# The first layer's output bias is added behind each chunk's norm, and the fourth chunk's transposes stand four side steps later

## The chip, the cores and the metric

The kernel runs on one core of a Trainium2 chip. The metric is the device time in microseconds of one execution. Three executions of the kernel before took 730.15, 731.93 and 731.92 us, median 731.92 us.

## The reference

Two transformer layers on an input `x` of 2 x 1024 tokens of width 256, all float32. Each layer normalizes `x`, feeds the result to an attention and to a gated feed-forward block, and adds both to `x`:

```python
xn = _layernorm(x)
x = x + _L0_attn_ref(xn, ...) + _L0_ffn_ref(xn, ...)
xn = _layernorm(x)
x = x + _L1_attn_ref(xn, ...) + _L1_ffn_ref(xn, ...)
```

The part around the change is layer 0. Its attention is linear, with 16 heads of 16, and its last operation adds a bias row `o_b` to every token:

```python
qp = elu(q) + 1.0;  kp = elu(k) + 1.0
kv = einsum('bhsd,bhse->bhde', kp, v)
z = einsum('bhsd,bhd->bhs', qp, kp.sum(axis=2))[..., None]
attn = einsum('bhsd,bhde->bhse', qp, kv) / (z + EPS)
return out @ o_w.T + o_b
```

Its feed-forward block uses three ternary weights, `clip(round(w / s), -1, 1) * s` with `s` the mean of `|w|`, as `down(silu(up(x)) * gate(x))`. Layer 1 has softmax attention with rotary positions and a Hadamard-rotated feed-forward block; the change does not touch it.

## The kernel before, in words

The 2048 tokens are four chunks of 512, held in `X` as 16 tiles of 128 tokens on the partitions. Every float32 product is done in two or three float32r passes, with operands split in a high and a low part (`XH`, `XL` for the normalized input, `W0H`, `W0L` for the weights of layer 0).

All engines run one list of pieces that `work_order` writes out. Each engine walks the same list and issues only its share of each piece; semaphores hold them together. So the place of a piece in the list sets the order on every engine at once. Generators feed the list: `layernorm` (one per chunk), `ternary` (one per ternary weight), `attention0` through `side0`, and `ffn` as the main loop. The start of the kernel, before `half` and the first `gate`, is written by a short loop of `FIRST` = 12 side steps. The change is in that loop.

The pieces that matter here:

- `ln_stats n`: VectorE takes mean and variance of chunk n (L1128, L1132, L1135), and GpSimd raises the variance to the power -0.5 (`rstd`, L1592).
- `ln_norm n`: VectorE writes the normalized chunk to `XC` in four instructions (L1144), out of `X`.
- `ln_turn n`: TensorE transposes the four tiles of `XC` (L807), ScalarE copies the two banks to `XH` (L1437), VectorE subtracts that from the banks to get `XL` (L1150). This is "the norm's turn".
- `bias 0 c`: GpSimd adds the row `OB` to the chunk c in `X` (L1601, 128x1024). It waits for the load of `OB` and for the chunk's four `ln_norm` instructions, since these read `X`.
- `kv_in t`, `kv_sum t`, `kv_out t`: key and value projection of token tile t. TensorE projects, VectorE adds biases (L1215 for `zk`, L1216 for `ve`, each from a bank in PSUM and the row `BKV` in SBUF), ScalarE makes the exponential (`ek`, L1454 and L1456), VectorE combines `zk` and `ek` (L1235, both in SBUF), and TensorE accumulates keys times values (L841). The banks 0 and 1 are used in turn.
- `q0 c m`: half of the query projection of a chunk. VectorE L1230, ScalarE `zs` (L1466, L1468), GpSimd adds the two (`QP`, L1613, both in SBUF).
- `tern_abs n`, `tern_scale n`, `tern_cut n j`: the ternary weight n (`TU`, `TG`, `TD`). ScalarE sums absolute values (L1446), VectorE makes the threshold (L1173 to L1176), compares all 2048 columns with it (L1178), and finishes in two halves (L1186, both inputs in SBUF).
- `gate`, `up` of the feed-forward block: ScalarE L1508, VectorE L1267 and L1280, then ScalarE rounds the product to `hh` (L1516), and GpSimd makes its low part `hl` (L1646, both inputs in SBUF).

GpSimd also adds the bias for layer 1 in the same place of each later norm (`bias 1 c` in `ln1`); that is not changed.

Of the kernel before, what the change touches and what calls it, by code (L numbers as in the profile page):

```python
# [49 lines left out]
class Ring:  # L50
# [5 lines left out]
    def next(self):  # L56
        self.i = (self.i + 1) % len(self.slots)
        return self.slots[self.i]
# [12 lines left out]
def work_order():  # L71
# [3 lines left out]
    def put(*piece):  # L75
        order.append(piece)
# [217 lines left out]
    sd0 = side0()  # L294
    next(sd0)
    next(ln0[2])
    next(sd0)
    for n in range(FIRST):
        if n < 10:
            next(tn)  # L300
        next(sd0)
        if n < 4:
            next(ln0[2 if n == 0 else 3])
        if n > 7:
            put("bias", 0, n - 8)
    put("half")
    put("load_down")
    put("load_ob1")
# [138 lines left out]
def program(nc, x_d, wa0, tern, wa1, wo1, wf1, cols_d, bkv_d, cos_d, sin_d, had_d, mask_d, ident_d, pad_d, sel_d, wl_d, ob_d, wsd_d, y_d):  # L447
    with ExitStack() as ctx:
# [134 lines left out]
        def o_slots(p):  # L583
# [7 lines left out]
            return (f"oe{o}", n), (f"num{i}", done), (f"rc{o}", n), (f"rs{o}", n)  # L591

        order = work_order()
        block = ctx.enter_context(nc.Block())

# [1209 lines left out]
```

## Time and profile before

| | |
|---|---|
| median of three executions | 731.92 us |
| profiled execution, its own time | 732.69 us |
| its span | 730.9 us |
| TensorE busy | 699.4 us, 96% of the span |
| VectorE busy | 529.2 us, 72% |
| ScalarE busy | 432.9 us, 59% |
| GpSimd busy | 288.2 us, 39% |
| mean granted TensorE clock | 0.986 |

Busy shares are means over the whole span. In the page's slices TensorE is at nine tenths or more nearly everywhere but in the first four slices (0 to 73 us), where it is at seven or eight tenths and VectorE at seven or eight as well. The change lies in those slices. The 18 to 70 us stretch has to be read from the timeline and the chain of waits, one instruction at a time, since there the engines hand work to one another every few tenths of a microsecond.

### The profile page before, as it was taken

Reading aid. Unit: us, or ns where it says so; the run is one execution under the profiler, and the core shown is the slowest. Engines: PE = TensorE matmul, PEld = TensorE weight load, DVE = VectorE, ACT = ScalarE, POOL = GpSimd, SP = SyncE. Lnnn points to the kernel's source line nnn. Section 1 sums busy time; section 2 is a strip of 40 time slices with the busy share of each in tenths; the row PEclk is TensorE's granted clock in tenths of the full one; section 3 lists DMA queues with packets and bytes.
Section 4 is the critical chain, followed back from the end, with each engine's and each line's share of the span. In section 5 each row is a group of like instructions: output and inputs, shape, how many; then the busy total and the mean of one; then the engine's idle time right before and its main releaser. Section 6 shows DMA issues by size and latency. Waiting matters only on the chain.

```text
span 730.9 us, 11063 instructions
## 1 busy us (share of the span) xinstructions
PE 699.4 (96%) x4246; PEld 441.5 (60%) x4246; DVE 529.2 (72%) x864; ACT 432.9 (59%) x592; POOL 288.2 (39%) x261
## 2 busy tenths in 40 slices
PE   7787999989998999999999999999999999999998
PEld 6576898977776888677676773333333333333445
DVE  7878875655668677678778788888886388888315
ACT  3363434446543522432332338999998999999883
POOL 2237944348665632542543431122333224332410
PEclk8999999989999999999999999999999999999999
DMA  7157001012025562423111022344443344433321
GB/s 266 55 187 231 1 1 58 1 26 91 1 87 173 167 208 87 144 70 105 59 59 35 25 67 71 126 140 160 123 143 126 100 146 146 145 94 91 105 79 58
DMA packets 25848, 74.14 MB, mean 101 GB/s; under 512 B 4620, under 2 KB 5996, under 8 KB 24964
## 3 DMA queue, kind: packets, MB, share of 16 engines
q1 hardware_dynamic: 21268, 65.37, 26.9%
q0 software_dynamic: 3808, 7.60, 3.6%
q8 instruction: 34, 0.56, 0.3%
q10 hardware_dynamic: 720, 0.48, 0.2%
q14 instruction: 18, 0.15, 0.1%
HBM read 54.54 MB, written 23.06 MB: 106 GB/s over the span
## 4 chain that ended last, share of the span: by engine, by line
PE 78%; DVE 10%; issue 5%; ACT 4%; POOL 3%; DMA 1%; DVEq 0%; ACTq 0%; POOLq 0%
PE PS L769 22%; PE PS L1038 17%; PE PS L1024 12%; PE PS L775 12%; PE PS L1007 6%; PE PS L997 5%; DVE mx L1342 1%; DVE bst L1128 1%; PE PS L903 1%; PE PS L858 1%; POOL hl L1646 1%; DVE sg L1280 1%; DVE rot L1325 1%; ACT XD L1432 1%; DMA X<-in_x 1%
## 5 line engine op out<-in xcount | busy, mean ns | idle before, releaser
L1554 ACT ACTIVATE P<-PS 128x1024 f32<-128x1024 f32 x256 | 249.0, 1024 | 30.0 <-PE PS L1024 29.7
L1349 DVE TENSOR_REDUCE mx<-PS 128x1 f32<-128x512 f32 x300 | 189.1, 682 | 32.3 <-PE PS L1007 30.6
L1342 DVE TENSOR_REDUCE mx<-PS 128x2 f32<-128x1024 f32 x106 | 124.8, 1220 | 36.6 <-PE PS L997 36.3
L1038 PE MATMUL PS<-P,VV 128*32 128x512 f32 x1024 | 136.4, 605 | 0.1
L1646 POOL TENSOR_TENSOR hl<-sg,hh 128x512 fp32r<-128x512 f32 x64 | 85.2, 1332 | 126.1 <-ACT hh L1524 75.8
L1024 PEld LDWEIGHTS PS<-QS,KS 64*128 64x128 f32 x512 | 48.4, 183 | 121.3 <-ACT P L1554 109.5
L1024 PE MATMUL PS<-QS,KS 64*128 64x512 f32 x512 | 116.4, 455 | 0.9 <-DVE mx L1342 0.6
L1007 PE MATMUL PS<-KM,QM 64*128 64x512 f32 x300 | 81.0, 395 | 0.0
L1510 ACT ACTIVATE sg<-PS,cols 128x512 f32<-128x512 f32 x32 | 22.0, 688 | 86.9 <-PE PS L769 86.9
L769 PE MATMUL PS<-XH,UGH 128*128 128x512 f32 x128 | 54.4, 425 | 3.7 <-DVE sg L1278 2.0
L769 PE MATMUL PS<-XL,UGH 128*128 128x512 f32 x128 | 50.5, 394 | 0.0
L769 PE MATMUL PS<-XH,UGL 128*128 128x512 f32 x128 | 50.0, 391 | 0.0
L1516 ACT ACTIVATE hh<-sg 128x512 fp32r<-128x512 f32 x32 | 20.1, 630 | 49.3 <-DVE sg L1280 49.3
L1655 POOL TENSOR_TENSOR sg<-sg,us 128x512 f32<-128x512 f32 x24 | 30.9, 1286 | 35.7 <-ACT us L1519 35.7
L1038 PEld LDWEIGHTS PS<-P,VV 128*32 128x32 f32 x1024 | 20.2, 108 | 39.8 <-issue 35.3
L997 PE MATMUL PS<-KM,QM 64*128 64x512 f32 x212 | 39.9, 448 | 0.8 <-DVE mx L1342 0.6
L1007 PEld LDWEIGHTS PS<-KM,QM 64*128 64x128 f32 x300 | 38.0, 185 | 3.4 <-DVE mx L1349 0.6
L775 PE MATMUL PS<-DH,hh 128*128 128x256 f32 x128 | 38.0, 297 | 0.0
L775 PE MATMUL PS<-DL,hh 128*128 128x256 f32 x128 | 36.1, 282 | 0.0
L775 PE MATMUL PS<-DH,hl 128*128 128x256 f32 x128 | 36.1, 282 | 0.0
L769 PEld LDWEIGHTS PS<-XH,UGH 128*128 128x128 f32 x128 | 24.0, 188 | 19.6 <-issue 10.8
L775 PE MATMUL PS<-TD,hh 128*128 128x256 f32 x128 | 34.0, 300 | 1.6 <-POOL hl L1646 1.6
(212 smaller groups left out, 1358.6 us busy)
## 6 DMA issues: line engine op xcount, KB each, us to landing
QM<-scr_q SPq DMA_DIRECT2D x16, 512.0 KB, 4.3
KM<-scr_k SPq DMA_DIRECT2D x16, 512.0 KB, 5.3
QS<-scr_q SPq DMA_DIRECT2D x16, 512.0 KB, 4.5
KS<-scr_k SPq DMA_DIRECT2D x16, 512.0 KB, 5.4
scr_q<-spl SPq DMA_DIRECT2D x24, 256.0 KB, 3.2
scr_k<-spl SPq DMA_DIRECT2D x24, 256.0 KB, 3.4
scr_o<-OE POOLq DMA_DIRECT2D x14, 256.0 KB, 2.8
stg<-in_tern SPq DMA_DIRECT2D x3, 1024.0 KB, 6.1
```

Of the source, the lines that this page charges most:

```text
L769: i = e.matmul(out, l, r, start=start and j == 0, stop=stop and j == len(pairs) - 1)
L775: i = e.matmul(out[:, r * 256:r * 256 + 256], l, x, start=first and r == 0 and j == 0, stop=last and j == len(pairs) - 1, skip_group_check ...
L997: e.matmul(bank[b + h], QM[p % 2][hr, qt * 128:(qt + 1) * 128], KM[p % 2][hr, chunk(half)], start=True, stop=True).then_inc(q["mt"], 1)
L1007: e.matmul(bank[b], QM[p % 2][hr, qt * 128:(qt + 1) * 128], KM[p % 2][hr, chunk(half)], start=True, stop=True).then_inc(q["mt"], 1)
L1024: i = e.matmul(bank[b + h], KS[p % 2][hr, kt * 128:(kt + 1) * 128], QS[p % 2][hr, chunk(half)], start=True, stop=True)
L1038: i = e.matmul(PS[32 * c:32 * c + 32, 7, :], v_head(8 * b + kt, 2 * j + c // 2), P[s % 4][:, chunk(c // 2 + 2 * (c % 2))], start=(kt == 0) ...
L1342: e.tensor_reduce(mx[p % 2][:, :, qt, half], PS[:, b:b + 2, :], AX.X, ALU.max).then_inc(q["mx"], 2)
L1349: e.tensor_reduce(mx[p % 2][:, h, qt, half:half + 1], bank[b], AX.X, ALU.max).then_inc(q["mx"], 1)
L1510: e.activation(s[:, :], bank[b], ACT.Silu, scale=col("wsg", m) if layer else su).then_inc(q["t"], 1)
L1554: e.activation(P[s % 4][:, half * 1024:(half + 1) * 1024], PS[:, b:b + 2, :].rearrange("p b n -> p (b n)"), ACT.Exp).then_inc(q["ex"], 1)
L1646: e.tensor_tensor(hl[f % 4][:, :], sg[f % 3][:, :], r32(hh[f % 4][:, :]), ALU.subtract).then_inc(q["hl"], 1)
L1655: e.tensor_tensor(s[:, :], s[:, :], us[f % 4][:, :], ALU.mult).then_inc(q["h"], 1)
```

## The change

The list of pieces is the same but for the places of five of them. The first three biases stand right behind `ln_norm 2`, where chunks 0 and 1 have long been normalized; the fourth stands behind `ln_norm 3`. Before, the four stood at the end of the start, behind the query and key work. And `ln_turn 3` is put at step 6 of the loop and no more at step 3 (counted from 0): behind `kv_in 6`, and no more behind `q0 0 1`.

```diff
     next(sd0)
     next(ln0[2])
+    for c in range(3):
+        put("bias", 0, c)
     next(sd0)
     for n in range(FIRST):
         if n < 10:
             next(tn)
         next(sd0)
-        if n < 4:
+        if n in (0, 1, 2, 6):
             next(ln0[2 if n == 0 else 3])
-        if n > 7:
-            put("bias", 0, n - 8)
+        if n == 2:
+            put("bias", 0, 3)
     put("half")
```

The changed file is two lines longer, so that the lines of the engines' code have numbers two higher in it (L1603 is the old L1601).

The first place is on GpSimd, from the third norm's `rstd` to the first `hl`. `X<-X,OB` is the bias; `QP` is the query add. Before:

```order
L1592 TENSOR_TENSOR rstd_144<-rstd_144,MINUS_HALF 128x4
L1592 TENSOR_TENSOR rstd_145<-rstd_145,MINUS_HALF 128x4
L1613 TENSOR_TENSOR QP<-zs_93,QP 128x512
L1613 TENSOR_TENSOR QP<-zs_94,QP 128x512
L1613 TENSOR_TENSOR QP<-zs_93,QP 128x512
L1601 TENSOR_TENSOR X<-X,OB 128x1024
L1613 TENSOR_TENSOR QP<-zs_94,QP 128x512
L1601 TENSOR_TENSOR X<-X,OB 128x1024 x3
L1646 TENSOR_TENSOR hl_110<-sg_118,hh_106 128x512
```

The same stretch now:

```order
L1594 TENSOR_TENSOR rstd_144<-rstd_144,MINUS_HALF 128x4
L1603 TENSOR_TENSOR X<-X,OB 128x1024 x3
L1594 TENSOR_TENSOR rstd_145<-rstd_145,MINUS_HALF 128x4
L1615 TENSOR_TENSOR QP<-zs_93,QP 128x512
L1603 TENSOR_TENSOR X<-X,OB 128x1024
L1615 TENSOR_TENSOR QP<-zs_94,QP 128x512
L1615 TENSOR_TENSOR QP<-zs_93,QP 128x512
L1615 TENSOR_TENSOR QP<-zs_94,QP 128x512
L1648 TENSOR_TENSOR hl_110<-sg_118,hh_106 128x512
```

Three biases moved ahead of the fourth norm's `rstd`, one between the first two query adds, and none is left ahead of `hl`.

The second place is on ScalarE, around the sum over the second ternary weight, `TG`. `XH` is the fourth norm's turn. Before:

```order
L1466 ACTIVATE zs1_94<-PS,MINUS_QB_62 128x512
L1468 ACTIVATE zs1_94<-zs1_94 128x512
L1437 ACTIVATE XH_68<-PS 128x512 x2
L1446 ACTIVATE TG_77,s16_53<-stg0_121 128x2048
L1454 ACTIVATE ek0_84<-zk0_80 128x256
L1456 ACTIVATE ek0_84<-ek0_84 128x256
L1454 ACTIVATE ek1_85<-zk1_81 128x256
L1456 ACTIVATE ek1_85<-ek1_85 128x256
L1454 ACTIVATE ek2_86<-zk2_82 128x256
L1456 ACTIVATE ek2_86<-ek2_86 128x256
L1454 ACTIVATE ek3_87<-zk3_83 128x256
```

Now:

```order
L1468 ACTIVATE zs1_94<-PS,MINUS_QB_62 128x512
L1470 ACTIVATE zs1_94<-zs1_94 128x512
L1448 ACTIVATE TG_77,s16_53<-stg0_121 128x2048
L1456 ACTIVATE ek0_84<-zk0_80 128x256
L1458 ACTIVATE ek0_84<-ek0_84 128x256
L1456 ACTIVATE ek1_85<-zk1_81 128x256
L1458 ACTIVATE ek1_85<-ek1_85 128x256
L1456 ACTIVATE ek2_86<-zk2_82 128x256
L1458 ACTIVATE ek2_86<-ek2_86 128x256
L1439 ACTIVATE XH_68<-PS 128x512 x2
L1456 ACTIVATE ek3_87<-zk3_83 128x256
```

The two copies to `XH` moved from ahead of the sum over `TG` to behind the exponentials of token tile 6 (`ek2`).

The third place is on VectorE, between the comparison of `TG` and its first half cut. Before:

```order
L1178 TENSOR_SCALAR TG<-stg_121,s_53 128x2048
L1215 TENSOR_TENSOR zk_82<-PS,BKV 128x256
L1216 TENSOR_TENSOR ve_90<-PS,BKV 128x2x128
L1235 SCALAR_TENSOR_TENSOR zk_81<-zk_81,ek_85 128x256
L1186 SCALAR_TENSOR_TENSOR TG<-stg_121,s_53,TG 128x1024
L1215 TENSOR_TENSOR zk_83<-PS,BKV 128x256
```

Now:

```order
L1180 TENSOR_SCALAR TG<-stg_121,s_53 128x2048
L1217 TENSOR_TENSOR zk_82<-PS,BKV 128x256
L1218 TENSOR_TENSOR ve_90<-PS,BKV 128x2x128
L1237 SCALAR_TENSOR_TENSOR zk_81<-zk_81,ek_85 128x256
L1152 TENSOR_TENSOR XL<-PS,XH 128x512 x2
L1188 SCALAR_TENSOR_TENSOR TG<-stg_121,s_53,TG 128x1024
L1217 TENSOR_TENSOR zk_83<-PS,BKV 128x256
```

The two subtractions for `XL` moved in ahead of the cut; they had stood ahead of the `zk` of token tile 4.

## Rows read from the trace of the kernel before

**Rows 1.** Busy time by stretch; columns: us, then PE, PEld, DVE, ACT, POOL, clock, DMA
```profile
80.00:100.00 20.00, 20.00 (x139) 18.59 (x138) 14.94 (x28) 6.18 (x12) 14.58 (x8) 1.00 0.01 1
```

**Rows 2.** Chain that ended last; columns: start us, us, engine and line
```profile
72.18 0.73 PE PS L858 x4
```

**Rows 3.** Timeline of GpSimd, 15 to 63 us; columns: start us, us, engine, line, operation
```profile
15.03 2.98 POOL L1592 TENSOR_TENSOR rstd<-rstd,MINUS_HALF 128x4 f32<-128x4 f32 x1 [4.62 <-DVE rstd L1135]
...
54.70 8.10 POOL L1601 TENSOR_TENSOR X<-X,OB 128x1024 f32<-128x1024 f32 x3
...
57.06 5.74 POOL L1601 TENSOR_TENSOR X<-X,OB 128x1024 f32<-128x1024 f32 x2
...
62.77 3.48 POOL L1646 TENSOR_TENSOR hl<-sg,hh 128x512 fp32r<-128x512 f32 x2
```

**Rows 4.** Timeline of VectorE, 20 to 26 us
```profile
20.91 1.37 DVE L1144 TENSOR_SCALAR XC<-X,mv,rstd 128x256 f32<-128x256 f32 x4
...
22.87 0.41 DVE L1235 SCALAR_TENSOR_TENSOR zk<-zk,ek 128x256 f32<-128x256 f32 x1
23.20 0.42 DVE L1215 TENSOR_TENSOR zk<-PS,BKV 128x256 f32<-128x256 f32 x1
...
23.87 0.41 DVE L1235 SCALAR_TENSOR_TENSOR zk<-zk,ek 128x256 f32<-128x256 f32 x1
25.03 1.29 DVE L1150 TENSOR_TENSOR XL<-PS,XH 128x512 fp32r<-128x512 f32 x2 [0.75 <-ACT XH L1437]
```

**Rows 5.** Timeline at 75.9 us, GpSimd and VectorE side by side
```profile
75.87 1.31 POOL L1646 TENSOR_TENSOR hl<-sg,hh 128x512 fp32r<-128x512 f32 x1
75.93 1.53 DVE L1235 SCALAR_TENSOR_TENSOR zk<-zk,ek 128x256 f32<-128x256 f32 x1
```

**Rows 6.** Instructions of L1144 and L1178; durations in ns, min/median/max
```profile
L1144 DVE TENSOR_SCALAR XC<-X,mv,rstd x16: 404/406/414, 9.0 to 33.9; 128x256 f32<-128x256 f32 x16
...
L1178 DVE TENSOR_SCALAR TG<-stg,s x1: 1287/1287/1287, 42.0 to 42.0; 128x2048 fp32r<-128x2048 f32 x1
```

**Rows 7.** Timeline of all engines, 34 to 42 us
```profile
34.26 2.43 POOL L1613 TENSOR_TENSOR QP<-zs,QP 128x512 f32<-128x512 f32 x1 [1.32 <-ACT zs L1468]
34.27 1.28 DVE L1186 SCALAR_TENSOR_TENSOR TU<-stg,s,TU 128x1024 fp32r<-128x1024 f32 x1
...
36.96 0.63 ACT L1468 ACTIVATE zs<-zs 128x512 f32<-128x512 f32 x1
37.50 1.07 ACT L1437 ACTIVATE XH<-PS 128x512 fp32r<-128x512 f32 x2
...
38.45 1.91 ACT L1446 ACTIVATE TG<-stg 128x2048 fp32r<-128x2048 f32 x1
...
41.24 0.42 DVE L1235 SCALAR_TENSOR_TENSOR zk<-zk,ek 128x256 f32<-128x256 f32 x1 [0.18 <-ACT ek L1456]
```

**Rows 8.** Timeline of ScalarE and VectorE, the third turn and the cut of TG
```profile
24.10 0.42 ACT L1456 ACTIVATE ek<-ek 128x256 f32<-128x256 f32 x1
...
24.42 1.07 ACT L1437 ACTIVATE XH<-PS 128x512 fp32r<-128x512 f32 x2
...
44.12 0.42 ACT L1456 ACTIVATE ek<-ek 128x256 f32<-128x256 f32 x1
...
44.22 1.28 DVE L1186 SCALAR_TENSOR_TENSOR TG<-stg,s,TG 128x1024 fp32r<-128x1024 f32 x1
```

**Rows 9.** Timeline of VectorE and ScalarE, 57 to 66 us
```profile
57.93 2.62 DVE L1178 TENSOR_SCALAR TD<-stg,s 128x2048 fp32r<-128x2048 f32 x1
...
60.47 0.68 DVE L1280 TENSOR_TENSOR sg<-sg,PS 128x512 f32<-128x512 f32 x1
...
61.17 0.63 ACT L1516 ACTIVATE hh<-sg 128x512 fp32r<-128x512 f32 x1 [3.03 <-DVE sg L1280]
...
62.94 2.17 DVE L1186 SCALAR_TENSOR_TENSOR TD<-stg,s,TD 128x1024 fp32r<-128x1024 f32 x1
...
65.03 0.68 DVE L1267 SCALAR_TENSOR_TENSOR sg<-sg,PS 128x512 f32<-128x512 f32 x1
```

## The prediction

> **What bounds the kernel now.** I read the stretches first, then the chain of waits, then the timeline of the stretch that the change touches. From 80 to 100 us TensorE is busy for 20.00 of 20.00 us [rows 1], and the page's slices keep it at nine tenths or so until the end. Up to there it isn't the bound: the chain of waits runs through VectorE, with pieces of ScalarE and GpSimd, and goes over to TensorE at 72.18 us [rows 2]. So I treat whatever moves that handover as moving the end by the same amount, and nothing that the change does lies behind it. The sum is therefore a walk from 18 to 72 us along VectorE and ScalarE. The times are those of the trace of before; "x late" means against it.
>
> What the walk needs most is how GpSimd and VectorE get in each other's way. At 75.87 GpSimd starts an add of two SBUF tiles, and at 75.93 VectorE starts its L1235, also with two SBUF inputs, and takes 1.53 us [rows 5] where it takes 0.41 alone [rows 4]. GpSimd's add ends at 77.18, L1235 at 77.46: it began in earnest about when the add was done, and ended 0.28 behind it. The same at 57.93: the comparison L1178 takes 2.62 us [rows 9] against 1.29 [rows 6], because a bias had begun at 57.06 [rows 3]. VectorE wins the other way round: at 34.27 it begins a cut, and GpSimd's query add takes 2.43 us [rows 7]. Instructions that read PSUM and one SBUF tile show no such stretching: L1280 at 60.47, beside a bias, takes its 0.68 [rows 9].
>
> **The biases at their new place.** The third norm's rstd ends at 15.03 + 2.98 = 18.01 [rows 3]. The waits of the first two biases have long been met. A bias every 2.36 us (57.06 less 54.70 [rows 3]) gives starts at 18.0, 20.35 and 22.7; the third waits for the third norm, done at 22.28 [rows 4], so it doesn't wait. It ends at 25.06. VectorE reaches the first L1235 at 22.87 [rows 4], 0.17 behind it. With 0.06 ahead GpSimd had the port in [rows 5]. Then L1235 ends at 25.06 + 0.28 = 25.34 and not at 23.28, and what follows it is 2.07 late. Nothing absorbs that: the next L1215 at 23.20 feeds ScalarE's exponential, behind which stand XH and then XL at 25.03 [rows 4], where VectorE waits for ScalarE as it is. So +2.07.
>
> The other end: if the gap behind rstd, which no row shows, is 0.2 us or more, VectorE passes first. Its L1235 runs at 22.87, the third bias gets the port at about 23.1 and ends at 25.5, and it is the second L1235, at 23.87, that is held to 25.8. XL follows at 25.72 and not at 25.03: +0.70. I take +2.07, since 0.17 is more than the 0.06 that did for GpSimd in [rows 5], and keep +0.70.
>
> **The fourth bias.** It stands behind the first query add, which ended at 34.26 + 2.43 = 36.69 [rows 7], so it runs from 36.7 to 39.1 (all plus the shift so far). It holds up the L1235 of tile 3 until 39.3. Behind that stand L1215 and L1216 of tile 5, two thirds of a microsecond at 0.33 each, so that VectorE is ready for the next L1235 at 39.9. That one needs ScalarE's exponential, which by the next paragraph is there at 40.3. Cost 0, with 0.4 to spare; if that cover goes, up to 2.
>
> **The turn, where it leaves.** Before, ScalarE goes from the exponential of zs (36.96) to the two XH copies at 37.50 and to the sum over TG at 38.45 [rows 7]. Now the sum starts at 37.50: 0.95 sooner. All behind it follows: the exponentials of tile 4, the L1235 that waits for them (41.24 with 0.18 of idle time before it [rows 7]), the threshold, the comparison of TG. By the paragraph above VectorE can follow to 40.29. TensorE gets its key work for tile 4 sooner, since it no longer waits there for the fourth norm, so it holds nobody. So -0.95. VectorE's two XL instructions leave idle time there, which is worth nothing.
>
> **The turn, where it comes in.** VectorE has to do the two XL between the L1235 of tile 5 and the first cut of TG at 44.22 [rows 8]. They need XH, which stands on ScalarE behind the exponential of tile 6 that begins at 44.12. Such an XH begins 0.32 behind the start of the exponential (24.10 to 24.42) and XL 0.61 behind XH (24.42 to 25.03 [rows 4, 8]), so XL at 44.12 + 0.93 = 45.05. Two XL keep VectorE for 1.21 (1.29 less the overlap with what follows), and the cut starts at 46.26: +2.04. From there to the handover VectorE and ScalarE work through the cuts, the query adds and the sum over TD in line, so nothing gives it back. Together the turn costs 1.09. The lower bound of this term is 0 for the arrival (it would be hidden if VectorE had 2 us to wait there, which [rows 8] deny), the upper one 2.04 plus what a later bank costs TensorE, which has the keys of tile 7 to do meanwhile and is not waited for.
>
> **The biases at their old place.** Three of them kept GpSimd from 54.70 to 62.80 [rows 3]. Two instructions of VectorE paid. The comparison for TD took 2.62 at 57.93; at 1.29 it saves 1.33, and L1280 at 60.47, hh at 61.17 and the cut at 62.94 move up by as much [rows 9]. That cut took 2.17 because two hl had piled up behind the biases and started at 62.77 [rows 3]; alone it takes 1.28 [rows 8], a saving of 0.89. Not all of it: the second hl can now begin 0.07 behind its hh, at 61.17 - 1.33 + 0.63 + 0.07 = 60.54, takes 1.31 [rows 5], and ends at 61.85, while the cut wants the port at 61.61. By the end of L1235 in [rows 5] VectorE gets going some 0.13 ahead of the recorded end, so that costs about 0.11, and 0.78 stay. So -1.33 - 0.78 = -2.11, and L1267 at 65.03 is up by as much. Nothing of GpSimd's stands behind this but the hl, fold and butterfly pieces in their old order.
>
> **Sum.** +2.07 - 0.95 + 2.04 - 1.33 - 0.78 = +1.05. The profiled execution took 732.69, 0.77 above the median of 731.92. On its own scale the kernel comes to 733.7, on that of the median to 733.0 us.
>
> **Rivals.**
>
> (1) VectorE slips ahead of the third bias. For it: 0.17 us is all the room there is, and no row shows how soon GpSimd starts something behind an rstd. Against it: other adds of GpSimd follow one another without a gap (54.70 + 2.36 = 57.06). Sum: 0.70 in place of 2.07, hence -0.32 and 731.6 us.
>
> (2) Slower: the norm's own instructions are held by the biases too. At 20.91 VectorE begins four XC instructions while the second bias runs, until 22.7. Held up to there, they end at 24.0; the third bias waits for them and runs from 24.05 to 26.4; L1235, reached at 24.5, ends at 26.7. What follows it is then 3.45 late and not 2.07, the sum +2.4, the time 734.3 us. It decides if XC takes more than 0.41 beside a bias. Against it: sixteen XC lie between 404 and 414 ns [rows 6], those of the first norm beside a GpSimd rstd. But that one is 4 columns wide, so it is no full proof. The Trainium skill, in "SBUF — State Buffer", section "Who interferes with whom", lists tensor_scalar among the operations that can enter a mode that takes both ports of VectorE, and says that whichever engine issues first has the shared pair for the whole instruction; by that the XC would be held and the time would be this rival's, and by its sentence that an instruction with one SBUF input outside such a mode doesn't contend, it would be my forecast. The trace speaks for the second: L1144 needs 1.37 us for 4 x 256 columns [rows 4], L1178 1.29 for 2048 [rows 6], so L1144 runs at about half the pace of the one and is not in the fast mode.
>
> (3) Faster: the turn's arrival is hidden, because the chain at 43 to 48 us is in truth ScalarE's or TensorE's, and (1) as well. Sum -0.32 - 2.04 = -2.36, time 729.6 us. For it: VectorE idles in most microseconds of this stretch for a little. Against it: the cut at 44.22 begins with no idle time before it [rows 8].
>
> There is one more tie, at 34.26 and 34.27 [rows 7]: both engines shift alike there, so VectorE should win it again. If GpSimd does, VectorE's cut is late by a query add, about 1.1, in any of the cases.
>
> **Chances.** The forecast 0.42; (1) 0.26; (2) 0.10; (3) 0.10; the tie lost or something not seen 0.12, half to each side. What a measurement of this kernel can tell from no change is about 0.3%, 2.2 us. The forecast and (1) lie within it; (2) is just above, (3) just below it. That makes faster 0.15, same 0.69, slower 0.16. The range goes from just above (3) to just above (2), 729.8 to 734.7 us; the forecast's own is 732.2 to 733.7.
>
> **What would show it.** In the profile after: one L1237 near 22.9 us with 2.4 to 2.5 us of duration (forecast), or a second one at 23.9 with about 1.9 (rival 1); XC at 20.9 still at 0.41 each (else rival 2); the sum over TG 0.95 nearer to the exponential of zs; VectorE waiting 0.8 us for XH ahead of XL at about 46; no instruction of TD's comparison above 1.3 us and its first cut below 1.4; TensorE's first L860 behind which it stays busy at about 73.2 us and not 72.18. I am wrong if that handover moves by more than 2 us, or if it moves as said and the end doesn't follow.

## The result: slower by 4.1 us

| | before | after |
|---|---|---|
| median | 731.93 us (5 runs, 730.15 to 732.48) | 735.98 us (5 runs, 734.87 to 737.67) |
| profiled execution, its own time | 732.69 us | 736.19 us |
| span | 730.9 us | 734.3 us |
| handover to TensorE | 72.18 us | 75.06 us |

The ratio is 1.0058, with a 95% interval of 1.0039 to 1.0077. The forecast was 733.0 us with a range of 729.8 to 734.7, and 0.16 for "slower by over 0.3%". That is what came, and the median lies outside the range.

VectorE's timeline from the second norm's `XL` to `XL` of the third, in the profile after. Columns: start us, us, engine, line, operation.

```profile
16.84 1.28 DVE L1152 TENSOR_TENSOR XL<-PS,XH 128x512 fp32r<-128x512 f32 x2
18.03 2.14 DVE L1165 TENSOR_SCALAR s<-cols 128x2 f32<-128x2 f32 x1
20.09 0.16 DVE L1166 TENSOR_SCALAR s16b<-cols 128x8 f32<-128x8 f32 x1
20.16 2.31 DVE L1167 TENSOR_SCALAR MINUS_QB<-cols 128x2 f32<-128x2 f32 x1
22.38 0.16 DVE L1169 TENSOR_SCALAR MASK<-MASK 128x8 f32<-128x8 f32 x1
22.46 0.41 DVE L1217 TENSOR_TENSOR zk<-PS,BKV 128x256 f32<-128x256 f32 x1
...
23.12 1.37 DVE L1146 TENSOR_SCALAR XC<-X,mv,rstd 128x256 f32<-128x256 f32 x4
...
25.08 2.14 DVE L1237 SCALAR_TENSOR_TENSOR zk<-zk,ek 128x256 f32<-128x256 f32 x1
27.15 0.41 DVE L1217 TENSOR_TENSOR zk<-PS,BKV 128x256 f32<-128x256 f32 x1
...
28.98 1.29 DVE L1152 TENSOR_TENSOR XL<-PS,XH 128x512 fp32r<-128x512 f32 x2 [0.76 <-ACT XH L1439]
```

And GpSimd's timeline in the same stretch and at the biases' old place:

```profile
17.76 4.69 POOL L1603 TENSOR_TENSOR X<-X,OB 128x1024 f32<-128x1024 f32 x2
24.57 2.37 POOL L1603 TENSOR_TENSOR X<-X,OB 128x1024 f32<-128x1024 f32 x1 [2.12 <-DVE XC L1146]
...
60.76 1.29 POOL L1648 TENSOR_TENSOR hl<-sg,hh 128x512 fp32r<-128x512 f32 x1 [1.41 <-ACT hh L1518]
65.62 1.28 POOL L1648 TENSOR_TENSOR hl<-sg,hh 128x512 fp32r<-128x512 f32 x1 [3.58 <-ACT hh L1518]
```

Four things are to be seen. L1165 and L1167, two tensor_scalar instructions 128x2 wide of the piece `signs`, take 2.14 and 2.31 us beside the first two biases; the eight-column L1166 slips between the two biases at 0.16. So the first key add (L1217) comes at 22.46, where it came at 20.24 before. The four XC at 23.12 come after the second bias, so no bias runs beside them in this profile, and the third bias waits for them. It starts at 24.57, half a microsecond ahead of the key sum L1237 at 25.08, which then takes 2.14 us where it takes 0.41 alone; that is the hold forecast for the key sum at the old 22.87 [rows 4]. And the hl of GpSimd start at 60.76 and 65.62, right behind their hh, not in a heap as in [rows 3].

The rest of the start, where each line answers to one of [rows 7 to 9]:

```profile
41.09 2.18 DVE L1237 SCALAR_TENSOR_TENSOR zk<-zk,ek 128x256 f32<-128x256 f32 x1
...
44.23 0.45 DVE L1237 SCALAR_TENSOR_TENSOR zk<-zk,ek 128x256 f32<-128x256 f32 x1 [0.29 <-ACT ek L1458]
...
48.07 1.29 DVE L1152 TENSOR_TENSOR XL<-PS,XH 128x512 fp32r<-128x512 f32 x2 [0.76 <-ACT XH L1439]
49.28 1.28 DVE L1188 SCALAR_TENSOR_TENSOR TG<-stg,s,TG 128x1024 fp32r<-128x1024 f32 x1
```
```profile
40.92 0.63 ACT L1470 ACTIVATE zs<-zs 128x512 f32<-128x512 f32 x1
41.46 1.90 ACT L1448 ACTIVATE TG<-stg 128x2048 fp32r<-128x2048 f32 x1
...
47.14 0.42 ACT L1458 ACTIVATE ek<-ek 128x256 f32<-128x256 f32 x1
47.46 1.06 ACT L1439 ACTIVATE XH<-PS 128x512 fp32r<-128x512 f32 x2
```
```profile
62.99 1.28 DVE L1180 TENSOR_SCALAR TD<-stg,s 128x2048 fp32r<-128x2048 f32 x1
64.19 0.68 DVE L1282 TENSOR_TENSOR sg<-sg,PS 128x512 f32<-128x512 f32 x1
...
66.67 1.32 DVE L1188 SCALAR_TENSOR_TENSOR TD<-stg,s,TD 128x1024 fp32r<-128x1024 f32 x1
67.91 0.67 DVE L1269 SCALAR_TENSOR_TENSOR sg<-sg,PS 128x512 f32<-128x512 f32 x1
```

The first fence is VectorE around the comparison of TG, the second ScalarE beside it, the third VectorE at TD. The sum over TG starts 0.54 behind the exponential, without the XH copies between. VectorE waits for XH before XL at 48.07, and the cut of TG comes at 49.28. TD's comparison takes 1.28 and its first cut 1.32 us.

Each step can be read off as the lateness of one instruction against the first profile, and the difference from one row to the next is what the step cost:

| what | before | after | late | step | forecast |
|---|---|---|---|---|---|
| first key add, L1215 | 20.24 | 22.46 | +2.22 | +2.22 | 0 |
| key add of tile 2 | 23.20 | 27.15 | +3.95 | +1.73 | +2.07 |
| key sum of tile 4, L1235 | 41.24 | 44.23 | +2.99 | -0.96 | -0.95 |
| first cut of TG, L1186 | 44.22 | 49.28 | +5.06 | +2.07 | +2.04 |
| L1280 behind TD's comparison | 60.47 | 64.19 | +3.72 | -1.34 | -1.33 |
| L1267 behind TD's cut | 65.03 | 67.91 | +2.88 | -0.84 | -0.78 |
| handover, L858 | 72.18 | 75.06 | +2.88 | 0 | 0 |
| an hh behind the handover, L1516 | 87.61 | 92.00 | +4.39 | +1.51 | 0 |
| an hh behind the fifth norm, L1516 | 166.37 | 169.82 | +3.45 | -0.94 | 0 |

The last two steps go with TensorE's clock; for the first of them an experiment below shows it, the second was not tested. TensorE by stretches of the profile after; columns: stretch and its us, then PE, PEld, DVE, ACT, POOL busy with instructions, granted clock, DMA share, GB/s. First the handover:

```profile
75.06 1.27 PE L860 MATMUL PS<-kvb,QP 128*128 128x136 f32 x4 [2.85 <-DVE at L1249]
```
```profile
76.00:80.00 4.00, 4.00 (x15) 3.21 (x15) 2.10 (x7) 0.95 (x2) 4.00 (x3) 0.71 0.00 0
```

TensorE had idled for 2.85 us and then had a mean granted clock of 0.71 over 76 to 80 us: part of that time it ran at 1.2 GHz and part at 2.4. A matmul of 512 columns took 0.63 us at the lower level where it took 0.39 in the profile before:

```profile
76.56 0.63 PE L771 MATMUL PS<-XL,TU 128*128 128x512 f32 x1
```
```profile
72.98 0.39 PE L769 MATMUL PS<-XL,TU 128*128 128x512 f32 x1
```

In the profile before, the idle time at this place was 1.42 us, and the stretch had clock 1.00:

```profile
76.00:80.00 4.00, 4.00 (x25) 3.55 (x24) 2.81 (x5) 2.25 (x5) 4.00 (x3) 1.00 0.01 4
```

The same thing the other way round stands at the fifth norm: ten microseconds of it in the profile before, and the ten of the same work, 4 us later, in that after:

```profile
154.00:164.00 10.00, 8.75 (x42) 7.58 (x41) 4.37 (x11) 3.30 (x7) 3.75 (x3) 0.66 0.15 31
```
```profile
158.00:168.00 10.00, 8.53 (x45) 7.47 (x46) 5.24 (x14) 3.98 (x8) 4.30 (x3) 0.83 0.17 53
```

There the clock was 0.66 before and 0.83 after, and 0.94 us came back. From there to the end nothing moves by more than about 0.1 us; the span ends 3.4 us later.

### The profile page after: what moved, and what is told of

It reads as the page before. It is cut to its first block, busy times and chain, and to the rows that moved or that the text cites. A ratio compares the mean times of both kernels' runs of the same rounds, so it can differ in the third digit from the quotient of the medians.

```text
span 734.3 us, 11063 instructions
## 1 busy us (share of the span) xinstructions
PE 699.3 (95%) x4246; PEld 441.0 (60%) x4246; DVE 534.5 (73%) x864; ACT 432.8 (59%) x592; POOL 286.3 (39%) x261
## 4 chain that ended last, share of the span: by engine, by line
PE 76%; DVE 11%; issue 5%; ACT 4%; POOL 3%; DMA 1%; DVEq 0%; ACTq 0%; POOLq 0%
PE PS L771 21%; PE PS L1040 17%; PE PS L1026 12%; PE PS L777 11%; PE PS L1009 6%; PE PS L999 5%; DVE bst L1130 1%; DVE mx L1344 1%; PE PS L905 1%; PE PS L860 1%; DVE XL L1152 1%; POOL hl L1648 1%; DVE sg L1282 1%; DVE rot L1327 1%; ACT XD L1434 1%
## 5 line engine op out<-in xcount | busy, mean ns | idle before, releaser
L1040 PEld LDWEIGHTS PS<-P,VV 128*32 128x32 f32 x1024 | 20.2, 108 | 39.8 <-issue 35.3
```

The source lines that it names most:

```text
L1040: i = e.matmul(PS[32 * c:32 * c + 32, 7, :], v_head(8 * b + kt, 2 * j + c // 2), P[s % 4][:, chunk(c // 2 + 2 * (c % 2))], start=(kt == 0) ...
```

## The experiments

All were timed over 5 to 12 executions against the kernel before on the same chip. "Late" is again against the first profile of before.

**The biases alone.** The turn is left where it was.

```diff
+    for c in range(3):
+        put("bias", 0, c)
     next(sd0)
     for n in range(FIRST):
         ...
         if n < 4:
             next(ln0[2 if n == 0 else 3])
-        if n > 7:
-            put("bias", 0, n - 8)
+        if n == 2:
+            put("bias", 0, 3)
```

> The kernel before with the four biases at their new places, and the fourth turn where it was. Theory A (two small tensor_scalar instructions of the piece signs, 2 columns wide, and then one L1235 are held by the early biases): VectorE's first key add is late by 2.4 us, what follows the first L1235 by 4.2, the place where the bias left gives 2.2 back, so the handover to TensorE moves by +2.0 and the end by 2 to 3.5 us. Rival B (the turn's move is what costs): the handover moves by less than 0.5 us and the end too.

Measured: 734.6 us against 731.83, ratio 1.0038 [1.0023, 1.0053]. VectorE again shows the two held instructions, and the key sum:

```profile
18.42 2.15 DVE L1165 TENSOR_SCALAR s<-cols 128x2 f32<-128x2 f32 x1
...
20.55 2.31 DVE L1167 TENSOR_SCALAR MINUS_QB<-cols 128x2 f32<-128x2 f32 x1
...
25.47 2.15 DVE L1237 SCALAR_TENSOR_TENSOR zk<-zk,ek 128x256 f32<-128x256 f32 x1
```

TD's comparison takes 1.29 us. The handover comes at 74.36, +2.18 (forecast +2.0), and the span ends 2.5 us later. This profile runs 0.39 us behind that of the changed kernel already at L1165 (18.42 against 18.03); 2.18 - 0.39, and 1.10 for the turn (next experiment), make up the 2.88 of the changed kernel. So the biases cost most of it. Rival B falls.

**The turn alone.**

```diff
-        if n < 4:
+        if n in (0, 1, 2, 6):
             next(ln0[2 if n == 0 else 3])
```

> The kernel before with only the fourth turn moved. Theory A: the sum over TG starts 0.95 us sooner, the first cut of TG 1.1 later, the handover 1.1 later and the end 1 to 2.5 us later, all of it still in TD's comparison at 2.6 us. Rival B: the handover and the end move by 3 us or more.

Measured: 732.58 us against 731.83, ratio 1.0009 [0.9996, 1.0021]: 0.7 us, and the interval takes in nothing and 1.5. The profile has to be read with care, since the handover stands at 72.06, 0.12 sooner than before. But the first key add comes at 19.02 and not at 20.24, in code that is the same up to there. From the first key add to the handover it is 53.04 us here and 51.94 in the profile before: the turn costs 1.10, as the -0.96 and +2.07 above. What differs at the start is TensorE's clock, here in this kernel and then in the one before, over the same stretches:

```profile
14.00:16.00 2.00, 2.00 (x14) 2.00 (x13) 1.93 (x7) 2.00 (x4) 1.10 (x1) 0.68 0.28 115
16.00:18.00 2.00, 2.00 (x17) 1.91 (x16) 2.00 (x3) 1.54 (x2) 1.88 (x1) 1.00 0.00 0
```
```profile
14.00:16.00 2.00, 2.00 (x12) 2.00 (x11) 1.93 (x8) 2.00 (x4) 0.97 (x1) 0.50 0.31 127
16.00:18.00 2.00, 2.00 (x12) 2.00 (x12) 2.00 (x3) 1.64 (x2) 2.00 (x1) 0.57 0.00 0
```

Rival B falls. Theory A's 1 to 2.5 us at the end were not seen: the profile ends 0.2 us later, with the early start in it, and the size of the turn's cost in the median is only as sure as the interval.

**The changed kernel with `signs` out of the biases' way.**

```diff
-    for i in (0, 1, 0, 1, 0, 2):
+    for i in (0, 1, 0, 1, 0):
         next(ln0[i])
+    put("signs")
+    next(ln0[2])
 ...
     next(tn)
-    put("signs")
```

> The changed kernel with the piece signs (four small tensor_scalar instructions of VectorE) ahead of the third norm's statistics, where no bias runs. Theory A: they take 0.16 us each, the first key add comes at its old time of 20.2 us, and VectorE meets the third bias at its first L1235 as the prediction said, held there for about 2 us; the handover falls by 2.1 us against the changed kernel, the end by 2 to 3.5. It also puts the four XC instructions beside the second bias for the first time. Rival C (a bias holds any tensor_scalar with its input in SBUF): XC is held for 1.5 to 1.8 us too, and of the 2.1 us less than 0.8 are left. Rival B (signs stands beside the path): no change.

Measured: 735.29 us against 731.83, ratio 1.0052 [1.0038, 1.0067], hardly less than the changed kernel. `signs` is no more held, and the first key add comes at 19.09. But the XC are. Two rows of VectorE in narrow windows, and the second bias, with the third:

```profile
19.76 0.91 DVE L1147 TENSOR_SCALAR XC<-X,mv,rstd 128x256 f32<-128x256 f32 x1
```
```profile
20.59 2.45 DVE L1147 TENSOR_SCALAR XC<-X,mv,rstd 128x256 f32<-128x256 f32 x1
```
```profile
20.48 2.41 POOL L1604 TENSOR_TENSOR X<-X,OB 128x1024 f32<-128x1024 f32 x1
23.77 2.35 POOL L1604 TENSOR_TENSOR X<-X,OB 128x1024 f32<-128x1024 f32 x1 [0.88 <-DVE XC L1147]
```

The first XC takes 0.91, up to the end of the first bias, and the second 2.45, up to the end of the second bias that started 0.11 ahead of it; the last two take 0.4 each. The third bias then stretches the key sum to 2.12. The handover comes at 74.24, 0.82 sooner than in the changed kernel and not 2.1. Theory A was right that a bias had held `signs` and wrong on the gain, since the hold only went over to the next instruction that needs the port; rival C comes near to what was seen. It is the mechanism of rival 2 of the prediction, with only the second XC held for long.

**The idle time at the handover filled.** The changed kernel, with eight matmuls of ones (16 instructions in the trace) in front of the attention step that waits there.

```diff
     def att_n(tt):
+        if tt == 3:
+            put("busy", 8, 4)
         put("att_n", tt, ps.next())
```

> The changed kernel with eight matmuls of ones (128x128, their result is written to a bank that is written anew afterwards) ahead of the attention step at the handover, where TensorE idled 2.85 us and then ran with a granted clock of 0.71 for 76 to 80 us. Theory D (the clock behind that idle time cost 1.3 to 1.5 us of the 3.5): the clock stays at 1.00 behind the handover, the ScalarE step at about 88 us comes 1.3 to 1.5 us sooner, and the end by 0.5 to 1.5 us. Rival E (the clock there costs nothing, since VectorE sets the pace until 90 us): the step at 88 us and the end stay within 0.3 us.

Measured: 735.05 us against 731.83, ratio 1.0044 [1.0029, 1.0058]; the changed kernel had 1.0058 in its own comparison. VectorE does the same up to the handover, at 75.08. Behind it the clock stays up, and the hh of the table comes at 90.50 and not at 92.00:

```profile
75.08 0.73 PE L862 MATMUL PS<-kvb,QP 128*128 128x136 f32 x4 [0.74 <-DVE at L1251]
```
```profile
76.00:80.00 4.00, 4.00 (x24) 3.45 (x23) 3.49 (x8) 1.81 (x4) 4.00 (x2) 1.00 0.02 4
```
```profile
90.50 0.63 ACT L1520 ACTIVATE hh<-sg 128x512 fp32r<-128x512 f32 x1 [1.91 <-DVE sg L1284]
```

So 1.50 us between the handover and that hh were the clock. Up to 703 us 1.4 to 1.5 of them are left (2.0 late and not 3.4 to 3.5); at 722 us TensorE then waits 0.47 for VectorE, and the span ends 1.0 sooner than that of the changed kernel (733.3 and 734.3). The profiled execution took 735.12 and not 736.19. The medians differ by 0.9 us, with intervals that overlap. Theory D holds, rival E falls.

**The kernel before once more.**

> The kernel before, unchanged, for a second profile. In its first profile TensorE's granted clock was 0.50 to 0.57 from 12 to 18 us and the first key add came at 20.2 us; in two of the experiments the clock rose sooner and the first key add came at 19.0 to 19.1. Theory F (the point at which the clock rises at the start differs from execution to execution, and nothing else does): the time is within 0.2% of before, and if this profile has the clock up at 16 us, the handover to TensorE comes at about 71 us and not at 72.2. Rival G (the start is the same in each execution of this kernel): first key add at 20.2 again.

Measured: 732.08 us against 731.86, ratio 0.9995 [0.9979, 1.0011]. The first key add came at 20.35 and the handover at 72.31, the clock being 0.50 at 16 to 18 us. So both profiles of this kernel have the late start, as rival G says, and theory F is not shown. The turn alone, whose code is the same up to there, had the early one, but that is another program. The 23 executions of before that this one was compared with lie between 730.07 and 734.60 us, so something differs from one execution to the next; no profile shows that it is this. This execution took 734.03 us: 1.0 of that is a stretch near 247 us, which the other profiles lack.

**The biases in the gaps.** The kernel before, the turn as it was.

```diff
     for n in range(FIRST):
         ...
+        if n == 0:
+            put("bias", 0, 0)
         if n < 4:
             next(ln0[2 if n == 0 else 3])
-        if n > 7:
-            put("bias", 0, n - 8)
+        if n == 2:
+            put("bias", 0, 1)
+        if n in (8, 9):
+            put("bias", 0, n - 6)
 ...
             def bias(layer, c):
                 e.wait_ge(q["lnn"], 4 * (4 * layer + c + 1))
+                if layer == 0 and c == 0:
+                    e.wait_ge(q["kvk"], 2)
```

> The kernel before with its biases set where VectorE does nothing that a bias holds: chunk 0 behind the second key sum (GpSimd waits for it, about 24.3 to 26.7 us), chunk 1 between the first two query adds (36.7 to 39.1), chunks 2 and 3 where the first two stood. The turn stays. Theory A (only instructions that need the shared port pay): no instruction of VectorE before 50 us is longer than before by more than 0.2 us, but for 0.3 us at the key sum of tile 3; TD's comparison takes 1.3 us and its first cut under 1.4; the handover comes 2.0 to 2.2 us sooner than before, and the median falls by 1.5 to 2.5 us, to 729.5 to 730.5. Rival H (the early biases cost through something else than the port, as the waits of the query adds): the handover moves by less than 1 us.

Measured: 730.09 us against 731.86, ratio 0.9969 [0.9954, 0.9984], 12 and 23 runs: faster than both kernels. GpSimd with its four biases, and VectorE at the instructions that could pay:

```profile
24.54 2.38 POOL L1607 TENSOR_TENSOR X<-X,OB 128x1024 f32<-128x1024 f32 x1 [6.65 <-issue]
...
36.79 2.37 POOL L1607 TENSOR_TENSOR X<-X,OB 128x1024 f32<-128x1024 f32 x1
...
51.26 2.40 POOL L1607 TENSOR_TENSOR X<-X,OB 128x1024 f32<-128x1024 f32 x1
...
54.87 2.39 POOL L1607 TENSOR_TENSOR X<-X,OB 128x1024 f32<-128x1024 f32 x1
57.23 1.27 POOL L1652 TENSOR_TENSOR hl<-sg,hh 128x512 fp32r<-128x512 f32 x1
```
```profile
26.80 1.29 DVE L1182 TENSOR_SCALAR TU<-stg,s 128x2048 fp32r<-128x2048 f32 x1
...
40.13 0.56 DVE L1239 SCALAR_TENSOR_TENSOR zk<-zk,ek 128x256 f32<-128x256 f32 x1
...
58.09 1.49 DVE L1182 TENSOR_SCALAR TD<-stg,s 128x2048 fp32r<-128x2048 f32 x1
...
61.97 1.33 DVE L1190 SCALAR_TENSOR_TENSOR TD<-stg,s,TD 128x1024 fp32r<-128x1024 f32 x1
```

The first bias ends at 26.9, and the comparison L1182 comes at 26.80 with its usual 1.29; the key sum of tile 3 pays 0.15, TD's comparison 0.2, because the first hl now stands right ahead of it. The handover is at 70.37, -1.81 (forecast -2.0 to -2.2), and the end -2.6. Theory A holds, with a little less than it promised, and rival H falls: an early bias costs next to nothing where VectorE does nothing that needs the port.

**The clock in all profiles.** One can follow the same hh as in the table above through every profile, with the mean granted clock over the same work: about 16 us from the handover to the hh at 87.61 of before, and the ten at the fifth norm. "Step" is the change in lateness over that stretch.

| profile | TensorE idle before the handover | clock behind it | step | clock at the fifth norm | step |
|---|---|---|---|---|---|
| before | 1.42 | 1.00 | | 0.66 | |
| after | 2.85 | 0.90 | +1.51 | 0.83 | -0.94 |
| biases alone | 2.85 | 0.91 | +1.42 | 0.83 | -0.97 |
| `signs` moved | 2.83 | 0.83 | +2.77 | 1.00 | -2.39 |
| idle time filled | 0.74 behind the added matmuls | 1.00 | -0.01 | 0.83 | -0.87 |
| biases in the gaps | 2.85 | 1.00 | 0 | 0.83 | -0.87 |
| turn alone | 1.33 | 1.00 | +0.01 | 0.66 | +0.43 |
| before once more | 1.31 | 1.00 | -0.01 | 0.66 | +0.10 |

The steps go with the clock at both places. The same idle time of 2.85 us cost 0, 1.4 and 1.5 us, and one of 2.83 cost 2.8; and the fifth norm gave something back to every kernel whose handover had moved by more than 0.2 us. Only the step behind the handover was tested by an experiment.

## Why the prediction was wrong

**What bounds the kernel.** Right: the path ran through VectorE to the handover, and what moved that moved the end. Wrong: "by the same amount". The handover moved by 2.88 and the work behind it by 4.39 at first and 3.45 in the end, by TensorE's clock; filling its idle time took 1.50 of that away. By the prediction's own sign ("I am wrong if that handover moves by more than 2 us") the walk itself was off, and not only what lies behind it.

**The biases at their new place.** This is the step that failed. The prediction took the first L1235 at 22.87 as the first instruction of VectorE that an early bias would meet. Between 18.0 and 22.87 stood `signs` and the four XC, and a bias can hold both. In the changed kernel it held `signs`, which pushed the XC behind the second bias; with `signs` out of the way it held the XC. `signs` was nowhere in the working, since at 0.16 us an instruction it looks like nothing; two of its four instructions cost 2.22 us at the first key add. The XC were in rival 2, at 0.10, and were argued away. The held L1235 itself was right in kind, with +1.73 for +2.07. The 0.34 less is there because the third bias, which waited for XC, started 0.5 us ahead of it and not 0.17. The room of 0.17 us for rival 1 played no part.

**Rival 2 and the argument against it.** I read from 4 x 256 columns in 1.37 us that L1144 is not in the mode that takes both ports, and so can't be held. That conclusion is wrong. In the experiment with `signs` moved, an XC beside a bias took 2.45 us. Its pace alone doesn't tell whether a tensor_scalar needs the port: L1165 does with two columns. The rule of the Trainium skill ("SBUF — State Buffer", section "Who interferes with whom"), that tensor_scalar is among the operations that can enter a mode that takes the shared pair, fits what the runs showed, in numbers 2.45 and 0.41 us with and without a bias; whether the XC is in that mode no run shows. Where a page says of an operation that it can be held and no row shows it beside the other engine at full width, the page should have had the larger chance. Had I priced `signs`, 2.2 in front of the 2.07, the sum would have been 3.3 and the time 735.2.

**The fourth bias.** Right: beside it the L1235 of tile 3 took 2.18 us at 41.09, and VectorE still waited 0.29 for the next one at 44.23.

**The turn.** Right in both halves, -0.96 and +2.07 for -0.95 and +2.04.

**The biases at their old place.** Right: -1.34 and -0.84 for -1.33 and -0.78.

**The sum.** At the handover +2.88 for +1.05: +2.22 that was left out, -0.34 at L1235, and -0.05 over the rest. At the end +3.4 to 3.5. The medians moved by 4.05. What of the remaining half microsecond is chance isn't settled; one cause that would go that way is in the start. Where no bias holds `signs`, the first key add waits for TensorE, and came at 19.0 to 19.1 in two profiles and at 20.2 to 20.4 in three, as TensorE's clock rose early or late. In the changed kernel it waits for `signs`, and came at 22.46, though TensorE began its first projection for it sooner (changed kernel, then the kernel before):

```profile
16.97 0.50 PE L771 MATMUL PS<-W0H,XH 128*128 128x512 f32 x1 [0.76 <-DVE W0L L1160]
```
```profile
18.50 0.47 PE L769 MATMUL PS<-W0H,XH 128*128 128x512 f32 x1
```

So the 2.22 us are measured against a late start, and an execution of before with an early one would lose another 1.2 by the change. Whether before has such executions was not shown, and how often was not measured.

**Rivals 1 and 3** did not occur. The tie at 34.26 came out as before: the query add beside the cut took 2.44 again.

## What to carry to other kernels

Before work is moved on one of two engines that share a port, list every instruction that the other one issues in the new window, the two-column ones too, since what is held costs what is left of the holder and not its own length. A tensor_scalar whose operands are all in SBUF belongs on that list whatever its pace. When a hold is taken from one instruction, the next that needs the port may inherit it; work is nearly free only in a window that has none. At the handover four such windows gave 1.8 us here where the four early places, taken alone, cost 2.2. Where TensorE idles before a handover, its clock behind it can add to the move: 0 to 2.8 us here for the same idle time.

## What the runs showed of the hardware that was not expected

- A tensor_scalar of 128x2 elements, SBUF to SBUF, took 2.14 and 2.31 us beside a GpSimd add and 0.16 alone. Yet two instructions 128x1 wide, SBUF to SBUF as well, took no longer than alone beside the bias that had begun at 57.06 [rows 3], in the profile before:

```profile
57.68 0.15 DVE L1175 TENSOR_SCALAR s<-s 128x1 f32<-128x1 f32 x1
57.75 0.14 DVE L1176 TENSOR_SCALAR s<-s 128x1 f32<-128x1 f32 x1
```

The Trainium skill ("VectorE: DVE Perf Modes", section "Mode 2×_2P — use both read ports for one tensor") says that the mode splits the access pattern in two halves along its outermost dimension, one for each port. With one column there is nothing to split, and these rows agree, with 0.15 and 0.14 us against 2.14 for two columns.

- Between two GpSimd instructions that follow one another without a gap, a VectorE instruction that was waiting got in: with `signs` moved, the first XC ended right behind the first bias, after 0.91 us, though the second bias had begun, and the next XC was held by that. In the profile after, L1165 ended right behind the first bias in the same way, and L1167 was held by the second; whether the eight-column L1166 between them at 20.09 needs the port at all, no row shows.
- Behind 2.85 us of idle time TensorE ran at a mean clock of 0.71 over 76 to 80 us in the changed kernel; behind 2.83 us it ran at 0.50 over the same stretch with `signs` moved; and behind 2.85 us in the kernel with the biases in the gaps (at 70.37) the clock stayed at 1.00. What else decides it is not settled.
